# One program, two orders: VectorE's instructions in the step of an attention pass that has a ranking beside it

## The chip, the core and the metric

The kernel runs on one NeuronCore of one Trainium2 chip. The metric is the time of one execution on the device in microseconds. Five engines work side by side, each in the order of its own program: TensorE (PE; its weight loads are shown as PEld), VectorE (DVE), ScalarE (ACT), GpSimd (POOL) and SyncE (SP), which here only starts transfers. They wait for each other through semaphores: counters that an instruction raises when it ends, and that another waits on.

## The reference, cut to what matters

Four graph networks follow each other on 6250 nodes and 100000 edges, each with a residual and a layer norm. The first has two attention layers, of which the second (one head of 64 columns) is the stage that the change is in:

```
def _gat_layer(x, src, dst, W, a_src, a_dst, b, num_nodes):
    h = (x @ W).reshape(num_nodes, H, C)
    al_s, al_d = einsum(h, a_src), einsum(h, a_dst)
    logits = leaky_relu(al_s[src] + al_d[dst], 0.2)
    alpha = segment_softmax(logits, dst)        # exp(logits - max of the segment) / sum
    out = segment_sum(h[src] * alpha, dst)
...
x = layernorm(x + L0(x, edges))    # two layers like the above, edges grouped by dst
x = layernorm(x + L1(x, edges))    # two heads, edges grouped by src
x = layernorm(x + L2(x, edges))    # dot product attention, edges grouped by src
x = layernorm(x + L3(x, edges))    # two graph convolutions with batch norm
```

The kernel itself puts the edges in an order by windows of 128 nodes, once by dst and once by src, before it can sum over segments.

## The kernel before, in words

Nodes are held in 49 windows of 128. Edges are put into groups of 128, each belonging to one window; there are 832 groups, and eight of them make a batch, so an attention pass has 104 batches. For a batch, GpSimd gathers 8 x 128 table rows by indirect DMA, TensorE fetches each edge's node values by a matmul with a one-hot matrix (`of_node`), VectorE forms the logits (`meet`, `leak`), takes running maxima along and across the groups (`join`, `scan_forward`, `scan_back`, `row_scan_forward`, `row_scan_back`, `drop`, `widen`, `top`), with small transposes by TensorE between (`flat`, `ends`, `columns`, `back`), subtracts the maximum (`subtract`), ScalarE takes two exponentials (`weights`), VectorE multiplies the gathered rows by them (`weigh`, in four pairs), TensorE sums each group over the edges (`sums`), and VectorE adds each of the eight results to its window's accumulator (`add`, which waits for the add before it). The result of a group's add lies in a window whose number VectorE reads into registers once in four batches.

The order of all this is written out by hand, in one function per engine: `step` for TensorE, ScalarE and VectorE, `fetch` for SP. A step t handles pieces of four batches: the logits and maxima of batch t, the weighing and the first adds of batch t - 1, the last adds of t - 2, and the one-hot `turn` of t + 2.

In the second attention pass (stage `a2e`) another work runs beside it: the ranking of the edges by src, 98 batches of eight chunks of 128 edges (`SteppedRanking`, object `r`). Batch u of it runs in step t = u + 5 (LAG = 5). For it VectorE makes one-hot rows (`r.turn`, `r.mark_windows`), compares (`r.alike`), reads out what TensorE counted (`r.find_slot`, `r.find_column`, `r.find_row`) and then marks, for each of the eight chunks k, the column of every edge (`r.mark_column`, line L698: 128 x 832 elements, for TensorE's `put`, line L736). ScalarE compares (`r.compare`, L582) and makes the signs of the rows (`r.step_rows`, L706). TensorE does `r.starts` and `r.earlier` around `flat`, puts 0 and 1 of batch u - 1 behind `ends`, 2 and 3 behind `columns`, and 4 to 7 last in its step. VectorE's order in this stage is `step_beside`; the change touches nothing else.

SP's `fetch_both(t)` starts the place row of batch t, then waits until VectorE has done `top` of batch t - 2 (semaphore `s_peak`), and only then starts the flags, turns and the ranking's three transfers and goes on to the next step's place row. `turn(t + 2)` on VectorE waits for such a place row.

Lines on which the argument rests: L1639 `top` (writes `peak`), L1569 `sum_parts`, L1650 `subtract` (`argument`), L614 `r.alike`, L698 `r.mark_column`, L1544 `weigh`, L1556 `add`, L1575 and L1577 `meet`, L1583 `leak`, L1588 `join`, L1609 and L1614 the scans, L1533 `turn`, L1619 and L1624 the row scans, L680, L684, L690 and L691 the three `r.find`, L602 `r.turn`, L607 `r.mark_windows`, L1634 `widen`.

## Time and profile before

| what | value |
|---|---|
| median of 3 executions | 8981.2 us (8963.2 to 8990.8) |
| profiled execution: its time, its span | 8990.8 us, 8988.0 us |
| VectorE busy | 5885.6 us, 65% |
| TensorE busy | 5885.0 us, 65% |
| GpSimd busy | 5907.3 us, 66% |
| ScalarE busy | 4187.7 us, 47% |
| stage with the ranking beside it | about 2346 to 3581 us |

Busy shares over the whole span are averages over some twenty stages that have different limits, so none of them says what the stage of the change is bound by; this is read from the stage's own stretch. A row of the waits names the instruction that waited and what it waited for, as far as semaphore events show it; the time is idle time of the engine just before the instruction.

### The profile page before, as it was taken

The page shows a single profiled execution, that of the slowest core. Times are in us where ns is not written, and L with a number is a line of the kernel's source. Part 1 is how long each engine was busy: PE and PEld are TensorE (multiplying, and loading weights), DVE is VectorE, ACT ScalarE, POOL GpSimd, SP SyncE. Part 2 cuts the span into 40 slices and gives each one's busy share as a digit, 9 for nine tenths or more (in the row PEclk, how much of TensorE's full clock was granted, in tenths as well). Part 3 has the DMA queues.
Part 4 walks back from the last instruction along what each step waited for, and adds up shares of the span by engine and source line. Part 5 has one row for each costly group of instructions (what it writes and reads, how often), then busy time and mean ns, then how long its engine had stood idle before and what let it go on. Part 6 is the DMA issues. An engine that isn't in the chain of part 4 may idle for free. (4 is left out here: it accounts for less than half of the span.)

```text
span 8988.0 us, 137581 instructions
## 1 busy us (share of the span) xinstructions
PE 5885.0 (65%) x32642; PEld 4068.4 (45%) x32642; DVE 5885.6 (65%) x17613; ACT 4187.7 (47%) x12362; POOL 5907.3 (66%) x6034
## 2 busy tenths in 40 slices
PE   5776667777688787577776777777764444433336
PEld 3343344554555555344444445555453333333335
DVE  8998788888588887566666799899862222211113
ACT  6897533333477676333333344444433333333332
POOL 7897377775577665177774266666647777577773
PEclk9998867777578777777777899899985555555557
DMA  1333245553244443244443366566521222111111
GB/s 47 111 116 106 73 131 136 136 135 104 75 102 104 113 99 89 73 132 132 132 132 102 127 177 174 170 173 173 173 73 53 53 53 53 40 27 27 27 27 40
DMA packets 518706, 903.05 MB, mean 100 GB/s; under 512 B 149411, under 2 KB 258877, under 8 KB 517564
## 3 DMA queue, kind: packets, MB, share of 16 engines
q0 software_dynamic: 226304, 550.69, 23.5%
q1 hardware_dynamic: 291644, 343.69, 12.6%
q8 instruction: 301, 4.93, 0.2%
q14 instruction: 457, 3.74, 0.1%
HBM read 820.41 MB, written 73.07 MB: 99 GB/s over the span
## 5 line engine op out<-in xcount | busy, mean ns | idle before, releaser
L1292 POOL DMA_INDIRECT all_Y<-table,all_row x3328 | 3250.0, 977 | 1543.0 <-issue 956.0
L1835 POOL DMA_INDIRECT all_Y<-table,all_row x1664 | 1574.0, 946 | 547.5 <-issue 506.8
L1851 PE MATMUL g1e_ps_u<-all_Y,g1e_onehot 128*128 128x128 f32 x1664 | 428.8, 439 | 620.0 <-DMA all_Y<-table,all_row 452.8
L1851 PE MATMUL g2e_ps_u<-all_Y,g2e_onehot 128*128 128x64 f32 x1664 | 406.5, 426 | 641.2 <-DMA all_Y<-table,all_row 592.6
L1343 PE MATMUL be_ps_u<-all_Y,be_onehot 128*128 128x258 f32 x1664 | 655.7, 549 | 258.9 <-DVE all_acc L1556 252.4
L1879 DVE TENSOR_TENSOR all_acc<-all_acc,g1e_ps_u 128x128 f32 x832 | 238.8, 287 | 812.1 <-PE g1e_ps_u L1851 705.7
L1879 DVE TENSOR_TENSOR all_acc<-all_acc,g2e_ps_u 128x64 f32 x832 | 183.6, 221 | 866.3 <-PE g2e_ps_u L1851 759.7
L1343 PE MATMUL a1e_ps_u<-all_Y,a1e_onehot 128*128 128x264 f32 x1664 | 706.1, 554 | 5.1 <-DVE all_acc L1556 3.2
L1851 PEld LDWEIGHTS g1e_ps_u<-all_Y,g1e_onehot 128*128 128x128 f32 x1664 | 370.5, 328 | 678.2 <-issue 339.5
L1851 PEld LDWEIGHTS g2e_ps_u<-all_Y,g2e_onehot 128*128 128x128 f32 x1664 | 370.5, 328 | 677.3 <-issue 349.2
L1343 PEld LDWEIGHTS be_ps_u<-all_Y,be_onehot 128*128 128x128 f32 x1664 | 395.5, 266 | 483.6 <-issue 352.9
L1324 PE MATMUL te_ps_q<-all_X,te_turned 128*128 x1664 | 509.2, 435 | 154.4 <-DVE te_product L1594 131.6
L1343 PE MATMUL te_ps_u<-all_Y,te_onehot 128*128 128x264 f32 x1664 | 534.6, 437 | 74.3 <-DVE all_Y L1544 73.4
L638 POOL TENSOR_SCALAR all_acc<-all_Y,all_acc 128x128 f16<-128x128 f16 x392 | 489.4, 1259 | 45.1 <-DVE all_acc L625 35.1
L736 PE MATMUL a2e_rank_ps_p<-all_X 128*128 128x512 f16 (+1 forms) x1568 | 466.8, 449 | 0.2
L1324 PEld LDWEIGHTS te_ps_q<-all_X,te_turned 128*128 128x128 f32 x1664 | 330.5, 213 | 288.9 <-issue 244.0
L1343 PEld LDWEIGHTS a1e_ps_u<-all_Y,a1e_onehot 128*128 128x128 f32 x1664 | 383.4, 261 | 86.5 <-issue 14.1
L671 PE MATMUL rank_dst_ps_p<-all_acc 128*128 128x512 f16 (+1 forms) x1568 | 349.5, 344 | 106.8 <-POOL all_acc L638 106.5
L698 DVE TENSOR_SCALAR all_X<-all_Y,all_acc 128x832 f16<-128x832 f16 x784 | 385.6, 492 | 35.3 <-PE a2e_rank_ps_p L736 35.3
L1864 ACT ACTIVATE g1e_onehot<-g1e_distance 128x1024 f32<-128x1024 f16 x104 | 109.8, 1056 | 638.5 <-PE g1e_ps_u L1851 638.3
L1864 ACT ACTIVATE g2e_onehot<-g2e_distance 128x1024 f32<-128x1024 f16 x104 | 109.9, 1056 | 638.2 <-PE g2e_ps_u L1851 638.1
L1556 DVE TENSOR_TENSOR all_acc<-all_acc,te_ps_u 128x264 f32 x832 | 346.1, 416 | 82.5 <-issue 54.8
(555 smaller groups left out, 15616.4 us busy)
## 6 DMA issues: line engine op xcount, KB each, us to landing
all_Y<-table,all_row POOLq DMA_INDIRECT x4992
a1e_place_row<-places_dst SPq DMA_DIRECT2D x104, 256.0 KB
a2e_place_row<-places_dst SPq DMA_DIRECT2D x104, 256.0 KB
be_place_row<-places_src SPq DMA_DIRECT2D x104, 256.0 KB
te_place_row<-places_src SPq DMA_DIRECT2D x104, 256.0 KB
all_Y<-lows_dst SPq DMA_DIRECT2D x98, 256.0 KB
all_Y<-codes_dst SPq DMA_DIRECT2D x98, 256.0 KB
all_acc<-lows_src SPq DMA_DIRECT2D x98, 256.0 KB
```

Source lines behind the costliest of these rows:

```text
L638: pool.tensor_scalar(self.row1[b][:, k, :], self.kept.half16, self.row[b][:, k:k + 1], self.kept.other_t[:, t * 8 + k:t * 8 + k + 1], ALU. ...
L671: last = pe.matmul(ps[:, 0:a1 - a0], self.row1[b][:, k, :], self.column1[b][:, k, a0:a1], start=first, stop=final)
L698: dve.tensor_scalar(self.column1[b][:, k, :], self.kept.lane16, self.column[b][:, k:k + 1], self.kept.other_t[:, t * 8 + k:t * 8 + k + 1], ...
L736: last = pe.matmul(ps[:, 0:a1 - a0], self.row1[b][:, k, :], self.column1[b][:, k, a0:a1], start=first, stop=final)
L1292: pool.indirect_dma_start(out=rows[:, r, k, :], out_offset=None, in_=table, in_offset=bass.IndirectOffsetOnAxis(ap=order.row[:, t * 8 + k: ...
L1324: last = pe.matmul(ps_q[pair % 2][:, j * HC:(j + 1) * HC], turned[b][:, k * P:(k + 1) * P], queries[:, bass.ds(windows.at(windows_j, chunk ...
L1343: pe.matmul(ps_u[k % 4][:, 0:R], onehot[b][:, k, :], summand[:, b, k, :], start=True, stop=True).then_inc(s_summed, 1)
L1556: dve.tensor_tensor(mine, mine, ps_u[k % 4][:, 0:R], ALU.add).then_inc(s_added, 1)
L1835: pool.indirect_dma_start(out=rows[:, r, k, :], out_offset=None, in_=table, in_offset=bass.IndirectOffsetOnAxis(ap=order.row[:, t * 8 + k: ...
L1851: last = pe.matmul(ps_u[u][:, k * width:(k + 1) * width], onehot[b][:, k, :], rows[:, r, k, :], start=True, stop=True)
L1864: act.activation(onehot[t % MARKS][:, :, :], distance[:, :, :], ACT.Relu, scale=-1.0, bias=1.0).then_inc(s_onehot, 1)
L1879: dve.tensor_tensor(mine, mine, ps_u[(t - 1) % AHEAD][:, k * width:(k + 1) * width], ALU.add).then_inc(s_added, 1)
```

## The change

Only the order of VectorE's instructions in `step_beside` is changed. The marks of a ranking batch, which stood one by one between other instructions (0 and 1 at the end of a step, 2 to 7 spread over the first half of the next), now stand in pairs: 0 and 1 behind `widen`, 2 and 3 behind `top` of the same step, 4 and 5 in front of `scan_forward` of the next, 6 and 7 in front of its `row_scan_forward`. `weigh` of pair 0 becomes the first instruction of a step, the adds 4 to 7 stand between the short instructions of `meet`, `leak` and `join`, `turn(t + 2)` and `r.turn` move behind `r.find_row`, and `r.alike` in front of `subtract`.

```
                     if t == 0:
                         sum_parts(t, b)
-                    if late:
-                        r.mark_column(dve, u - 1, 2)
+                    weigh(t - 1, n, rp, 0)
                     add(t - 2, 4, -12, j)
-                    if late:
-                        r.mark_column(dve, u - 1, 3)
+                    meet(t, b, ring)
                     add(t - 2, 5, -11, j)
-                    weigh(t - 1, n, rp, 0)
-                    meet(t, b, ring)
+                    weigh(t - 1, n, rp, 1)
                     leak(t, b)
-                    if late:
-                        r.mark_column(dve, u - 1, 4)
-                    weigh(t - 1, n, rp, 1)
+                    add(t - 2, 6, -10, j)
                     join(t, b)
-                    add(t - 2, 6, -10, j)
-                    if late:
-                        r.mark_column(dve, u - 1, 5)
                     add(t - 2, 7, -9, j)
                     weigh(t - 1, n, rp, 2)
                     if late:
-                        r.mark_column(dve, u - 1, 6)
+                        r.mark_column(dve, u - 1, 4)
+                        r.mark_column(dve, u - 1, 5)
                     scan_forward(t, b)
                     fade_first(t - 1, n, -8, j)
-                    if late:
-                        r.mark_column(dve, u - 1, 7)
                     scan_back(t, b)
                     add(t - 1, 0, -8, j)
                     weigh(t - 1, n, rp, 3)
-                    turn(t + 2, b)
+                    if late:
+                        r.mark_column(dve, u - 1, 6)
+                        r.mark_column(dve, u - 1, 7)
                     row_scan_forward(t, b)
                     if now:
                         r.find_slot(dve, u)
                     add(t - 1, 1, -7, j)
                     row_scan_back(t, b)
-                    if then:
-                        r.turn(dve, u + 1)
                     if now:
                         r.find_column(dve, u)
                     add(t - 1, 2, -6, j)
                     drop(t, b)
                     if now:
                         r.find_row(dve, u)
+                    turn(t + 2, b)
                     add(t - 1, 3, -5, j)
                     if then:
+                        r.turn(dve, u + 1)
                         r.mark_windows(dve, u + 1)
                     widen(t, b)
                     if now:
                         r.mark_column(dve, u, 0)
+                        r.mark_column(dve, u, 1)
                     top(t, b)
+                    if now:
+                        r.mark_column(dve, u, 2)
+                        r.mark_column(dve, u, 3)
                     sum_parts(t + 1, n)
-                    if now:
-                        r.mark_column(dve, u, 1)
-                    subtract(t, b)
                     if then:
                         r.alike(dve, u + 1)
+                    subtract(t, b)
```

VectorE, from the writing of the peak over the end of one step into the next, before. In these rows "ISA" is an instruction on registers, which makes the address of the add behind it; the line numbers shown are the same in both programs.

```order
L1639 SCALAR_TENSOR_TENSOR a2e_peak<-a2e_flags,a2e_ps_r,a2e_widened 9x128
L1569 TENSOR_REDUCE a2e_spread<-a2e_ps_n 128x16
L698 TENSOR_SCALAR all_X<-all_Y,all_acc 128x832
L1650 TENSOR_TENSOR a2e_argument<-a2e_argument,a2e_ps_r 128x16
L614 TENSOR_TENSOR all_acc<-all_acc,all_Y 128x1024
L698 TENSOR_SCALAR all_X<-all_Y,all_acc 128x832
L1556 ISA
L1556 TENSOR_TENSOR all_acc<-all_acc,a2e_ps_u 128x66
L698 TENSOR_SCALAR all_X<-all_Y,all_acc 128x832
L1556 ISA
L1556 TENSOR_TENSOR all_acc<-all_acc,a2e_ps_u 128x66
L1544 TENSOR_TENSOR all_Y<-all_Y 128x2x64
```

The same place in the changed program:

```order
L1639 SCALAR_TENSOR_TENSOR a2e_peak<-a2e_flags,a2e_ps_r,a2e_widened 9x128
L698 TENSOR_SCALAR all_X<-all_Y,all_acc 128x832 x2
L1569 TENSOR_REDUCE a2e_spread<-a2e_ps_n 128x16
L614 TENSOR_TENSOR all_acc<-all_acc,all_Y 128x1024
L1650 TENSOR_TENSOR a2e_argument<-a2e_argument,a2e_ps_r 128x16
L1544 TENSOR_TENSOR all_Y<-all_Y 128x2x64
L1556 ISA
L1556 TENSOR_TENSOR all_acc<-all_acc,a2e_ps_u 128x66
L1575 TENSOR_TENSOR a2e_raw<-a2e_spread,all_Y 128x8
L1577 TENSOR_TENSOR a2e_argument<-a2e_spread,all_begins 128x8
L1556 ISA
L1556 TENSOR_TENSOR all_acc<-all_acc,a2e_ps_u 128x66
```

The first weighing (L1544) has moved up to directly behind the subtraction (L1650), and the two adds have short instructions between them and no mark.

VectorE, around the forward scan and the old place of `turn`, before:

```order
L1556 TENSOR_TENSOR all_acc<-all_acc,a2e_ps_u 128x66
L1544 TENSOR_TENSOR all_Y<-all_Y 128x2x64
L698 TENSOR_SCALAR all_X<-all_Y,all_acc 128x832
L1609 SCALAR_TENSOR_TENSOR a2e_forward<-a2e_flags,a2e_ps_l 9x128
L1564 ISA
L1564 TENSOR_TENSOR all_acc<-all_acc,a2e_fade 128x66
L698 TENSOR_SCALAR all_X<-all_Y,all_acc 128x832
L1614 SCALAR_TENSOR_TENSOR a2e_local<-a2e_flags,a2e_forward 9x128
L1556 TENSOR_TENSOR all_acc<-all_acc,a2e_ps_u 128x66
L1544 TENSOR_TENSOR all_Y<-all_Y 128x2x64
L1533 TENSOR_SCALAR a2e_turned<-a2e_place_row,all_lane_p 128x1024
L1619 SCALAR_TENSOR_TENSOR a2e_row_forward<-a2e_turns,a2e_ps_r 1x18
```

The same place in the changed program:

```order
L1556 TENSOR_TENSOR all_acc<-all_acc,a2e_ps_u 128x66
L1544 TENSOR_TENSOR all_Y<-all_Y 128x2x64
L698 TENSOR_SCALAR all_X<-all_Y,all_acc 128x832 x2
L1609 SCALAR_TENSOR_TENSOR a2e_forward<-a2e_flags,a2e_ps_l 9x128
L1564 ISA
L1564 TENSOR_TENSOR all_acc<-all_acc,a2e_fade 128x66
L1614 SCALAR_TENSOR_TENSOR a2e_local<-a2e_flags,a2e_forward 9x128
L1556 TENSOR_TENSOR all_acc<-all_acc,a2e_ps_u 128x66
L1544 TENSOR_TENSOR all_Y<-all_Y 128x2x64
L698 TENSOR_SCALAR all_X<-all_Y,all_acc 128x832 x2
L1619 SCALAR_TENSOR_TENSOR a2e_row_forward<-a2e_turns,a2e_ps_r 1x18
```

A mark no longer stands between the two scans, two stand where `turn` was. `turn` is now here, shortly before `widen`, in the changed program:

```order
L691 TENSOR_SCALAR all_acc<-all_acc 128x8
L1533 TENSOR_SCALAR a2e_turned<-a2e_place_row,all_lane_p 128x1024
L1556 ISA
L1556 TENSOR_TENSOR all_acc<-all_acc,a2e_ps_u 128x66
L602 TENSOR_SCALAR all_acc<-all_acc,all_lane_p 128x1024
L607 TENSOR_TENSOR all_acc<-all_Y 128x392
L1634 SCALAR_TENSOR_TENSOR a2e_widened<-a2e_flags,a2e_ps_r,a2e_local 9x128
L698 TENSOR_SCALAR all_X<-all_Y,all_acc 128x832 x2
L1639 SCALAR_TENSOR_TENSOR a2e_peak<-a2e_flags,a2e_ps_r,a2e_widened 9x128
```

Before, the same piece had neither L1533 nor L602 in it and one mark (L698) between L1634 and L1639 where there are two now.

## Rows read from the trace of the kernel before

**Rows 1.** Busy time by stretch (us; instructions), then clock, DMA share, GB/s.
```profile
core 0: us, PE busy (x) PEld busy (x) DVE busy (x) ACT busy (x) POOL busy (x), PEclk, DMA share, GB/s
2430.00:3560.00 1130.00, 934.27 (x8250) 627.26 (x8250) 979.91 (x4026) 822.60 (x2679) 801.90 (x769) 0.78 0.42 103
```

**Rows 2.** VectorE's waits from 2430 to 3560: total us, times, longest.
```profile
DVE a2e_turned L1533 <- DMA a2e_place_row<-places_dst: 47.9, 37, 15.3
DVE a2e_forward L1609 <- PE a2e_ps_l L1350: 40.4, 45, 1.6
DVE all_X L698 <- PE a2e_rank_ps_p L736: 35.3, 24, 1.8
DVE a2e_widened L1634 <- PE a2e_ps_l L1368: 14.4, 43, 0.7
DVE a2e_argument L1650 <- PE a2e_ps_r L1374: 6.5, 40, 0.2
```

**Rows 3.** TensorE's and ScalarE's waits in the same stretch.
```profile
ACT all_acc L582 <- DMA all_acc<-records: 178.8, 95, 3.7
...
PE a2e_ps_r L1358 <- DVE a2e_local L1614: 84.1, 93, 1.4
...
PE a2e_ps_r L1374 <- DVE a2e_peak L1639: 17.2, 44, 0.5
```

**Rows 4.** Timeline, VectorE, two steps: start us, duration us, instruction, [idle before].
```profile
2696.23 0.34 DVE L1639 SCALAR_TENSOR_TENSOR a2e_peak<-a2e_flags,a2e_ps_r,a2e_widened 9x128 f32<-9x128 bf16 x1
...
2701.32 0.40 DVE L1609 TENSOR_TENSOR_SCAN a2e_forward<-a2e_flags,a2e_ps_l 9x128 f32<-9x128 bf16 x1
...
2703.20 0.49 DVE L1533 TENSOR_SCALAR a2e_turned<-a2e_place_row,all_lane_p 128x1024 bf16<-128x1024 f16 x1 [0.31 <-DMA a2e_place_row<-places_dst]
...
2707.06 0.34 DVE L1639 SCALAR_TENSOR_TENSOR a2e_peak<-a2e_flags,a2e_ps_r,a2e_widened 9x128 f32<-9x128 bf16 x1
...
2713.69 0.41 DVE L1609 TENSOR_TENSOR_SCAN a2e_forward<-a2e_flags,a2e_ps_l 9x128 f32<-9x128 bf16 x1 [1.21 <-PE a2e_ps_l L1350]
...
2718.68 0.34 DVE L1639 SCALAR_TENSOR_TENSOR a2e_peak<-a2e_flags,a2e_ps_r,a2e_widened 9x128 f32<-9x128 bf16 x1
```

**Rows 5.** Timeline, TensorE, the same two steps.
```profile
2696.71 0.20 PE L1374 MATMUL a2e_ps_r<-all_ident,a2e_peak 9*128 9x9 f32 x1 [0.39 <-DVE a2e_peak L1639]
...
2700.39 0.27 PE L1350 MATMUL a2e_ps_l<-all_ident,a2e_joined 128*9 128x128 f32 x1 [0.36 <-DVE a2e_joined L1588]
...
2707.77 0.27 PE L1374 MATMUL a2e_ps_r<-all_ident,a2e_peak 9*128 9x9 f32 x1
...
2713.31 0.27 PE L1350 MATMUL a2e_ps_l<-all_ident,a2e_joined 128*9 128x128 f32 x1
```

**Rows 6.** Busy time by stretch, with the granted clock, in these steps.
```profile
2697.00:2702.00 5.00, 4.28 (x61) 3.32 (x61) 5.00 (x22) 3.92 (x13) 3.77 (x5) 1.00 0.68 174
2703.00:2706.00 3.00, 3.00 (x20) 1.83 (x17) 2.76 (x13) 2.50 (x9) 2.32 (x3) 0.50 0.16 26
2708.00:2713.00 5.00, 5.00 (x35) 3.27 (x34) 4.39 (x18) 3.70 (x11) 3.77 (x5) 0.50 0.67 156
```

**Rows 7.** Timeline, VectorE: alike, the register read's gap, a mark and an add.
```profile
2901.77 0.67 DVE L614 TENSOR_TENSOR all_acc<-all_acc,all_Y 128x1024 f16<-128x1024 f16 x1
2903.88 0.49 DVE L698 TENSOR_SCALAR all_X<-all_Y,all_acc 128x832 f16<-128x832 f16 x1 [1.44 <-PE a2e_rank_ps_p L736]
2904.29 0.22 DVE L1556 TENSOR_TENSOR all_acc<-all_acc,a2e_ps_u 128x66 f32 x1
```

**Rows 8.** Timeline, VectorE, the stage's early steps, without the ranking.
```profile
2371.71 0.17 DVE L1650 TENSOR_TENSOR a2e_argument<-a2e_argument,a2e_ps_r 128x16 f32<-128x16 f32 x1 [0.31 <-PE a2e_ps_r L1374]
2372.26 0.29 DVE L1544 TENSOR_TENSOR all_Y<-all_Y 128x128 f32<-128x128 f32 x1 [0.38 <-ACT all_Y L1468]
...
2379.30 0.23 DVE L1556 TENSOR_TENSOR all_acc<-all_acc,a2e_ps_u 128x66 f32 x1
2379.73 0.22 DVE L1556 TENSOR_TENSOR all_acc<-all_acc,a2e_ps_u 128x66 f32 x1 [0.21 <-PE a2e_ps_u L1343]
```

**Rows 9.** L1544 in the first attention pass, 1200 to 2200 us: idle before it, times.
```profile
PE a1e_ps_u L1343: 24.2, 12
issue: 24.1, 12
```

## The prediction

> **What bounds the kernel now.** I read the page's slices first (no engine is busy throughout, and different stages have different limits), then the table by stretches for the one stage that the change touches. It is the second attention pass with the ranking beside it, from about 2346 to 3581 us, 104 steps. The stretch from 2430 to 3560 us has both works in it and 96 steps, so a step takes 1130 / 96 = 11.77 us; VectorE is busy for 979.9 of the 1130 us, TensorE for 934.3, at a mean granted clock of 0.78 [rows 1]. VectorE and TensorE hand work back and forth in every step, so I then read whom VectorE waits for [rows 2], whom TensorE waits for [rows 3], and two whole steps in order of time [rows 4, 5].
>
> The reader is to see two segments. Segment A runs from the end of `peak` (L1639) to the start of the forward scan (L1609): TensorE transposes the peak back, does sums, four puts, and the next step's node and start matmuls, then the `flat` transpose (L1350) that the scan needs. Segment B runs from the forward scan to the end of the next `peak`; in it VectorE sets the pace and TensorE waits for it.
> - Segment A took 2701.32 - 2696.57 = 4.75 us where VectorE had no wait, and 2713.69 - 2707.40 = 6.29 us in the next step, with 1.21 us of waiting for `flat` [rows 4]. TensorE took 3.95 us from back to the end of `flat` in the first (0.36 of it a wait for `joined`) and 5.81 us in the second [rows 5]. The clock granted was 1.00 (2.4 GHz) there and 0.50 (1.2 GHz) here; it fell between the two, while TensorE waited for `local` [rows 6]. So A is VectorE's at the fast level and TensorE's at the slow one: VectorE waited there in 45 of 96 steps, 40.4 us in all [rows 2].
> - Segment B took 2719.02 - 2713.69 = 5.33 us without a wait [rows 4]. TensorE always arrives first in it: it waits for `local` in 93 of 96 steps, 84.1 us [rows 3].
>
> VectorE's own work is thus 4.75 + 5.33 = 10.08 us of the 11.77. The rest per step: 0.37 for the read of window numbers into registers (35.3 us, every fourth step; the view names TensorE's puts as releaser, but those are two steps old), 0.50 for the place row's DMA, 0.42 for `flat`, 0.15 for the fall's columns, 0.07 for the back transpose [rows 2], and 0.18 of slips under 0.15 us each. That makes B on average 5.33 + 0.50 + 0.15 + 0.09 = 6.07 and A the other 5.70.
>
> **The change part by part.** No instruction is added or removed; only VectorE's order changes. PE, ACT, POOL and SP keep theirs.
>
> 1. *Marks move from A to B.* A held marks 1 to 6, now it holds 2 to 5; B held 7 and 0, now 6, 7, 0, 1. A mark takes 0.41 us from its start to the next one's (2904.29 - 2903.88) [rows 7]. A's own work becomes 4.75 - 0.82 = 3.93, B's 5.33 + 0.82 = 6.15. (Two marks in a row might be up to 0.02 cheaper each; I count nothing.)
>
> 2. *The first weighing now stands right behind the subtraction.* It needs both exponentials of ScalarE, which need the subtraction's result. Before, alike, two marks and two adds lay between. The stage's early steps, which have no adds yet, show the naked price: argument starts at 2371.71, the weighing at 2372.26 with 0.38 us of idle time, where an instruction without a wait would have started some 0.08 before the end of the one ahead (2904.29 against 2903.88 + 0.49): 0.46 [rows 7, 8]. In 24 steps the register read stands there and covers it. Bounds: 0 (ScalarE's work hidden after all) to 0.46 in 72 steps; I take 0.46. Queued behind it are all of VectorE's adds, and `joined`, which TensorE's flat waits for.
>
> 3. *Register read behind a short instruction.* It now follows the subtraction (0.17 us), not alike (0.68). The gap was 1.44 behind alike [rows 7]; in the first attention pass, where it follows the subtraction, it is (24.2 + 24.1) / 24 = 2.01 [rows 9]. Bounds 1.44 and 2.01; I take 2.0, since that is the same order. The Trainium skill (DMA: Bandwidth & Descriptors, section "Latency and other measured facts") gives a load into registers a floor of about 0.6 us; by that figure alone the 24 gaps would be 1.4 us shorter each, some 33 us less, but both places in this trace are far above it, and the sum does not use it.
>
> 4. *Adds lose the mark that lay between them.* Each add waits for the add before it. Where two stand together the second starts 2379.73 - 2379.30 = 0.43 us after the first, with 0.21 of idle [rows 8]. In the new order the instructions between adds 4 and 5 fill about 0.29 us, between 6 and 7 about 0.23, between 1 and 2 about 0.31. That costs 0.14 + 0.20 in A and 0.12 in B. Bounds: nothing (if my count of filler is short) to these 0.46 a step; I take them.
>
> 5. *`turn(t + 2)` moves from behind the fourth weighing to behind find_row.* It waited for the place row's DMA in 37 steps, 47.9 us [rows 2]. SP issues that DMA only once it has seen the peak of the step before, so its arrival stands still against `peak`, while turn comes later: it started 2703.20 - 2701.32 - 0.31 = 1.57 us behind the scan [rows 4], and will start about 3.3 us behind it (two marks and eight short instructions more), 1.7 us later. One wait is 15.3 us long (two large loads stand in the queue ahead of that place row), the other 36 have a mean of (47.9 - 15.3) / 36 = 0.9. The long one keeps 13.6, of the others I keep 4 of 32.6 us: some 18 us stay, 30 go. Bounds: none goes, all 47.9 go.
>
> 6. *Waits for the fall's columns* (14.4 us in B) *and for back* (6.5 us, in A) [rows 2] go: between drop and widen there are now 0.8 us more work, and behind `peak` two marks and alike.
>
> New B: 6.15 + 0.12 + 18 / 96 = 6.46 against 6.07: +0.39 x 96 = **+37 us**. New A: where TensorE is late (45 steps) its time stands; where it was not, VectorE needs 3.93 + 0.46 + 0.34 = 4.73 instead of 4.75; in the 24 steps with a register read 3.93 + 2.0 + 0.34 = 6.27 instead of 4.75 + 1.44 = 6.19. There is one gain: TensorE waited for `peak` in only 44 steps [rows 3]; in the other 52 it came to the back transpose late, 0.37 instead of 0.14 us behind peak (2707.77 - 2707.40 against 2696.71 - 2696.57) [rows 4, 5]. With the longer B it is there in time: 0.23 x 52 = -12, +2 for the register steps (0.08 x 24), and -1 for the steps that were VectorE's: **-11 us**. Last, ScalarE: it waits for the record's DMA, 1.9 us in the mean and 3.7 at the longest [rows 3]; where that is latest its exponentials come later than the 0.46 above, now without cover. My estimate is eight steps by 0.4: **+3 us**. Together +37 - 11 + 3 = **+29 us**, in a profiled execution of 8990.8 us (span 8988.0): 9020. That execution is the slowest of the three; the median is 8981.2, so the forecast is **9010 us**, +0.3%.
>
> A difference under 0.3% (27 us) is about what a measurement of this kernel cannot tell from none, so this forecast stands on that border.
>
> **The rivals.**
> - *R1, the adds' spacing costs nothing, and the sum is near zero.* For it: my count of filler is rough, and VectorE may fetch ahead while an add waits. Against it: the 0.43 us stands in the trace with the same form of add. Then B is (6.34 - 6.07) x 96 = +26, A loses another 0.34 in the some 40 steps where VectorE sets it (-11 - 14 = -25), ScalarE +3: +4, so 8985 us.
> - *R2, the clock.* Segment B gets longer with the same matmuls in it, so TensorE is idler there; the trace has it at 0.50 right after such idle time [rows 6]. My new A is (5.70 x 96 - 11 - 24 x 6.27) / 72 = 5.36 us in a step without a register read. If each of these began at 1.2 GHz, it would be the second step's 6.29 less the late 0.23, 6.06: +0.70 x 72 = +50 on top of +29, so 9060 us. Against it: B's mean is 6.46 against 6.07, and most of the old B's waits were idle time as well. The Trainium skill (TensorE: Matmul & The Clock Gate, section "Why this matters for your kernels") says that idle gaps between bursts of matmuls bring the clock back to its lower level; by that rule the change leans this way.
> - *R3, faster: the place row was the real brake.* Were segment A to follow VectorE alone (TensorE at 2.4 GHz more often because the idle time before `local` shrinks by the mark that stood there, 0.41 of its 84.1 / 93 = 0.9 us), a step would be 4.73 + 6.27 and the register steps 1.54 more: 72 x 11.0 + 24 x 12.54 + 18 = 1111 us, against 1130: -19, so 8962 us; with the adds' 0.46 free as well -63, 8918 us. It decides once A, in the steps without a register read, falls below (1130 - 96 x 6.46 - 24 x 6.27) / 72 = 4.99 us, from the 5.36 above. Against it: TensorE's own matmuls in A are the same, 3.6 us at 2.4 GHz but 5.8 at 1.2 [rows 5].
> - *R4, the order does nothing because TensorE's chain absorbs it.* It would need B to be TensorE's; it waits there in 93 of 96 steps, so I give it little and count it under "same".
>
> **How the numbers follow.** Forecast case, +29 with +-15: 0.42. R1 0.22. R2 0.18. R3 0.12. R4 0.06. The forecast case lies half above the 0.3% bound; with all of R2 and a share of R1 that gives slower 0.46. Same: a bit under half of the forecast case, most of R1 and R4, part of R3: 0.38. Faster: 0.16. The likeliest case's own range is 8995 to 9025; the range for 8 in 10 reaches down into R3 and up into R2: 8952 to 9068.
>
> **What would show it.** In the profile after: the first weighing waits for ACT L1468 in about 70 steps, 0.3 to 0.4 us each; the idle time by the register read goes from 1.44 to 2.0; the wait for the place row falls to 15 to 20 us, those for the columns and for back to nearly nothing; the wait for `flat` grows from 40 to about 60 us or more, since VectorE comes to the scan sooner; TensorE's wait for `peak` appears in nearly all steps; steps of about 12.05 us. I am wrong if the stretch of both works is shorter than before, if the weighing does not wait, or if the clock in it leaves 0.75 to 0.80.

## The result, and the profile after

The kernel after takes 9038.8 us in the median of four runs (9013.1 to 9043.2), the kernel before 8984.0 on the same chip (8963.2 to 8990.8): a ratio of 1.0064 with a 95% interval of 1.0049 to 1.0080, so some 57 us slower. The forecast was 9010 us, +29 us, with a range of 8952 to 9068; the direction held, and half of the size is missing in it. The profiled execution of after took 9060.3 us (span 9058.5).

The stretch with both works in it, now 1206 us long for the same 769 gathers [rows 1 have 1130 for them]:

```profile
core 0: us, PE busy (x) PEld busy (x) DVE busy (x) ACT busy (x) POOL busy (x), PEclk, DMA share, GB/s
2430.00:3636.00 1206.00, 973.21 (x8257) 661.26 (x8256) 988.14 (x4029) 824.04 (x2680) 971.97 (x769) 0.74 0.39 96
```

VectorE has 8 us more to do and ScalarE 1; it is GpSimd whose busy time went from 801.9 to 972.0 us, with as many instructions. VectorE's waits there (total us, times, longest), against [rows 2]:

```profile
DVE a2e_forward L1609 <- PE a2e_ps_l L1350: 67.2, 70, 1.7
DVE a2e_raw L1575 <- DMA all_Y<-table,all_row: 59.0, 19, 4.5
DVE all_Y L1544 <- ACT all_Y L1468: 52.3, 96, 1.1
DVE a2e_turned L1533 <- DMA a2e_place_row<-places_dst: 14.3, 1, 14.3
DVE a2e_widened L1634 <- PE a2e_ps_l L1368: 0.7, 1, 0.7
```

and TensorE's, against [rows 3]:

```profile
PE a2e_ps_r L1374 <- DVE a2e_peak L1639: 129.1, 91, 16.0
PE a2e_ps_r L1358 <- DVE a2e_local L1614: 19.5, 64, 0.9
```

Four of these lines are what the prediction asked for: the wait for `flat` grew from 40 to 67 us, the place row's shrank to its one long piece, the one for the columns is gone, and TensorE is in time for `peak` in 91 of 96 steps instead of 44. The weighing (L1544) does wait for ScalarE, in 96 steps where some 70 were expected. The second line, `meet` (L1575) waiting for the gathered rows up to 4.5 us at a time, was in no part of the prediction. So I read GpSimd, which has only gathers to issue in this stage: before, then after, 2430 to 3540 us, with count, busy time, mean ns of one, and idle time ahead of them.

```profile
L1292 POOL DMA_INDIRECT all_Y<-table,all_row x767 | 799.8, 1043 | 310.2 <-issue 205.7 <-DVE all_Y L1544 104.5
```
```profile
L1292 POOL DMA_INDIRECT all_Y<-table,all_row x707 | 896.1, 1268 | 215.4 <-issue 196.8 <-DVE all_Y L1544 18.6
```

One gather instruction takes 1.27 us in the mean instead of 1.04, and 0.30 us passes between two. Eight a step need 8 x (1.043 + 0.30) = 10.7 us before, of a step of 11.77, and 8 x (1.268 + 0.30) = 12.54 after, where the step, from the sixth forward scan of the stage to the last, is (3642.62 - 2410.92) / 98 = 12.57. GpSimd used to wait for VectorE (104.5 us) and hardly does any longer (18.6 us): it is what bounds the stage. One of its long instructions and its neighbours (start, us):

```profile
2552.67 1.19 POOL L1292 DMA_INDIRECT all_Y<-table,all_row  x1 [0.30 <-issue]
2554.16 3.57 POOL L1292 DMA_INDIRECT all_Y<-table,all_row  x1 [0.30 <-issue]
2558.04 0.94 POOL L1292 DMA_INDIRECT all_Y<-table,all_row  x1 [0.30 <-issue]
```

VectorE at the same time:

```profile
2554.23 0.88 DVE L698 TENSOR_SCALAR all_X<-all_Y,all_acc 128x832 f16<-128x832 f16 x2
2555.05 0.34 DVE L1639 SCALAR_TENSOR_TENSOR a2e_peak<-a2e_flags,a2e_ps_r,a2e_widened 9x128 f32<-9x128 bf16 x1
2555.31 0.89 DVE L698 TENSOR_SCALAR all_X<-all_Y,all_acc 128x832 f16<-128x832 f16 x2
2556.12 0.19 DVE L1569 TENSOR_REDUCE a2e_spread<-a2e_ps_n 128x16 f32<-128x48 f32 x1
2556.24 0.67 DVE L614 TENSOR_TENSOR all_acc<-all_acc,all_Y 128x1024 f16<-128x1024 f16 x1
2556.84 0.15 DVE L1650 TENSOR_TENSOR a2e_argument<-a2e_argument,a2e_ps_r 128x16 f32<-128x16 f32 x1
...
2557.58 0.21 DVE L1556 TENSOR_TENSOR all_acc<-all_acc,a2e_ps_u 128x66 f32 x1
2560.72 0.17 DVE L1575 TENSOR_TENSOR a2e_raw<-a2e_spread,all_Y 128x8 f32<-128x8 f32 x1 [2.92 <-DMA all_Y<-table,all_row]
```

The gather that began at 2554.16 ended at 2557.73, 0.89 us behind 2556.84, the start of the first instruction behind the row mark 0, mark 1, `top`, mark 2, mark 3, sum, alike. An undisturbed one takes 0.94 in all, so this one seems to have done its work when the row was over. All 39 gathers over 3 us in the stretch end 0.88 to 0.91 us behind the start of that instruction. VectorE then waits 2.92 us for the late rows of the table.

### The profile page after: what moved, and what is told of

Its sections match the earlier page's. It is cut to its first block and busy times, and to the rows that moved or that the text cites. A ratio compares the mean times of both kernels' runs of the same rounds, so it can differ in the third digit from the quotient of the medians.

```text
span 9058.5 us, 137581 instructions
## 1 busy us (share of the span) xinstructions
PE 5911.9 (65%) x32642; PEld 4085.2 (45%) x32642; DVE 5896.6 (65%) x17613; ACT 4188.0 (46%) x12362; POOL 6066.1 (67%) x6034
## 5 line engine op out<-in xcount | busy, mean ns | idle before, releaser
L1292 POOL DMA_INDIRECT all_Y<-table,all_row x3328 | 3413.4, 1026 | 1469.4 <-issue 966.4
L1830 POOL DMA_INDIRECT all_Y<-table,all_row x1664 | 1570.1, 944 | 548.8 <-issue 506.5
L1544 DVE TENSOR_TENSOR all_Y<-all_Y 128x128 f32<-128x128 f32 (+1 forms) x728 | 377.7, 519 | 74.3 <-ACT all_Y L1468 54.6
L671 PE MATMUL rank_dst_ps_p<-all_acc 128*128 128x512 f16 (+1 forms) x1568 | 352.1, 347 | 104.5 <-POOL all_acc L638 104.1
L1343 PE MATMUL a2e_ps_u<-all_Y,a2e_onehot 128*128 128x66 f32 x1664 | 350.7, 348 | 90.8 <-DVE all_acc L1556 90.6
```

The source lines that it names most:

```text
L671: last = pe.matmul(ps[:, 0:a1 - a0], self.row1[b][:, k, :], self.column1[b][:, k, a0:a1], start=first, stop=final)
L1292: pool.indirect_dma_start(out=rows[:, r, k, :], out_offset=None, in_=table, in_offset=bass.IndirectOffsetOnAxis(ap=order.row[:, t * 8 + k: ...
L1343: pe.matmul(ps_u[k % 4][:, 0:R], onehot[b][:, k, :], summand[:, b, k, :], start=True, stop=True).then_inc(s_summed, 1)
L1544: dve.tensor_tensor(out[:, :, :, 0:C], rows[:, r, ks, value_c0:value_c0 + HC].rearrange("p k (h n) -> p k h n", h=H), bc(by, [P, 2, H, C]) ...
L1830: pool.indirect_dma_start(out=rows[:, r, k, :], out_offset=None, in_=table, in_offset=bass.IndirectOffsetOnAxis(ap=order.row[:, t * 8 + k: ...
```

## The experiments

Two readings were set against each other. V: the loss is VectorE's own order, as predicted. P: VectorE's rows of marks, that is several of them one directly behind the other, slow GpSimd's gathers. From f2 on P has a sharper form, R: any unbroken row of marks and of operations with two inputs in SBUF (the core's working memory) holds a gather until the row is over. Each run below stands beside its own measurement of the kernel before, which lay between 8962 and 8977 us and not at 8984; so where an expectation names a time, compare its distance from before. The table holds all twelve runs; "step" is from the sixth forward scan to the last by 98, "need" is what GpSimd's gathers take of a step by their mean length and 0.30 us, "L1575" the waits for late rows over the whole stage, its beginning included.

| kernel | ratio to before (95%) | step | need | gather mean | L1575: us, times |
|---|---|---|---|---|---|
| before | 1 | 11.77 | 10.74 | 1.043 | 12.2, 3 |
| after | 1.0064 (1.0049, 1.0080) | 12.57 | 12.54 | 1.268 | 72.6, 23 |
| e1_marks_back | 1.0017 (1.0007, 1.0026) | 11.85 | 11.83 | 1.179 | 46.1, 16 |
| e2_marks_alone | 1.0103 (1.0088, 1.0119) | 12.60 | 12.56 | 1.270 | 49.3, 14 |
| e3_no_pairs | 1.0024 (1.0014, 1.0035) | 11.87 | 11.16 | 1.095 | 13.4, 3 |
| e4_weigh_later | 1.0092 (1.0077, 1.0107) | 12.49 | 12.49 | 1.261 | 87.8, 25 |
| f1_one_gather_off | 1.0029 (1.0020, 1.0038) | 11.95 | 10.68 (seven) | 1.226 | 5.7, 1 |
| f2_alike_behind | 1.0109 (1.0093, 1.0124) | 12.62 | 12.60 | 1.275 | 95.9, 28 |
| f3_turn_late | 0.9958 (0.9944, 0.9971) | 11.28 | 10.96 | 1.070 | 14.9, 5 |
| f4_marks_behind_top | 0.9967 (0.9955, 0.9979) | 11.33 | 10.89 | 1.061 | 13.2, 5 |
| g1_weigh_first | 0.9953 (0.9940, 0.9967) | 11.28 | 10.98 | 1.073 | 13.2, 3 |
| g2_alike_ahead | 0.9961 (0.9948, 0.9975) | 11.44 | 11.36 | 1.120 | 25.2, 10 |
| g3_slot_ahead | 0.9930 (0.9917, 0.9944) | 11.06 | 10.66 | 1.032 | 12.7, 4 |
| g4_both | 0.9955 (0.9942, 0.9969) | 11.37 | 11.09 | 1.086 | 12.4, 3 |

**e1_marks_back**, after with the marks alone put back:

```
 weigh 0
+mark 2
 add 4
+mark 3
 meet, add 5, weigh 1, leak
+mark 4
 add 6, join
+mark 5
 add 7, weigh 2
-mark 4, mark 5
+mark 6
 scan_forward, fade_first
+mark 7
 scan_back, add 0, weigh 3
-mark 6, mark 7
...
-mark 0, mark 1
+mark 0
 top
-mark 2, mark 3
 sum_parts
+mark 1
 alike, subtract
```

> Kernel after, with the eight marks alone put back to where the kernel before has them relative to the scans and products (each by itself, marks 2 and 3 in the next step, behind the weighing); the weighing first, the adds spread, the late turn and alike ahead of subtract stay. Theory P (pairs): in the trace of after GpSimd's gather instructions take 1.6 to 2.0 us where they lie beside two marks in a row and 3.4 to 3.6 us beside four, and in 23 steps the logit addition (L1575) then waits 2.4 to 4.5 us for the gather; with the marks apart these go, so 8980 to 9005 us, GpSimd's mean gather back at 1.05 us, and the wait at L1575 under 15 us. Theory V (VectorE's own order, as predicted: ScalarE's weights waited for, register read, adds bound to each other): all of these stay, so 9020 to 9045 us.

8977.9 us beside 8962.2, +16 us: three quarters of the loss go with the marks' place, as P has it, and V's range is missed. But the mean gather is 1.179, not 1.05, and 16 late ones stay: pairs are not the whole of it, and step and need still agree (11.85, 11.83).

**e2_marks_alone**, before with the marks where after has them:

```
-mark 2
 add 4
-mark 3
 add 5, weigh 0, meet, leak
-mark 4
...
+mark 4, mark 5
 scan_forward
...
 weigh 3
+mark 6, mark 7
...
+mark 1
 top
+mark 2, mark 3
 sum_parts
-mark 1
 subtract, alike
```

> Kernel before, with the marks alone put where the kernel after has them (4 and 5 ahead of the forward scan, 6 and 7 behind the fourth weighing, 0 and 1 ahead of top, 2 and 3 behind it); nothing else moved. Theory P: the pairs alone do it, so 9025 to 9060 us, gather instructions of up to 3.6 us, and waits of over 2 us at L1575 in some 20 steps. Theory V: the weighing still stands behind two adds and waits little, the two marks moved give the stretch ahead of the scan what they take from the one behind it, so 8965 to 9000 us.

9053.2 beside 8962.2, +91 us. P's time holds as it was stated; by its distance from before it is more than P expected, and more than the whole change costs. The long gathers are there (up to 3.73 us), the waits over 2 us fewer than the some 20 expected (12). V's range is missed.

**e3_no_pairs**, after's stretches, but one short instruction between any two marks:

```
-mark 4, mark 5, scan_forward, fade_first, scan_back, add 0, weigh 3, mark 6, mark 7
+mark 4, add 7, weigh 2, mark 5, scan_forward, fade_first, mark 6, scan_back, add 0, mark 7, weigh 3
...
-widen, mark 0, mark 1, top, mark 2, mark 3, sum_parts, alike
+mark 0, widen, mark 1, top, mark 2, sum_parts, mark 3, alike
```

> Kernel after, with the marks in the same stretches of the step (four around widen and top, four around the forward scan) but never two in a row: one short instruction between any two (0 widen 1 top 2 sum 3 alike, and 4 seventh-eighth add 5 forward scan and fade 6 backward scan and add 7). Theory P: GpSimd gets in between two marks, the gathers of 3.4 us and the 23 late ones go, so 8990 to 9015 us. Theory V: VectorE does the same work in the same two stretches, one mark more is even put between forward scan and its successors, so 9030 to 9060 us.

8985.2 beside 8962.2, +23 us: by this distance P's range, not V's. GpSimd needs only 11.16 of the 11.87 us here, so what is left of the loss, 23 us, is VectorE's.

**e4_weigh_later**, after without the wait for ScalarE:

```
-weigh 0, add 4, meet, add 5, weigh 1
+add 4, meet, add 5, weigh 0, weigh 1
```

> Kernel after, with the first weighing alone moved behind add 4, meet and add 5, so that it no longer waits for ScalarE's weights (54.6 us over the 102 steps of the last stage in the profiled run). Theory P: VectorE is not what binds; the 0.4 us a step are waited elsewhere (for the flat scan input or the gather), so 9025 to 9045 us, within 15 us of after. Theory V: the wait is on the path in some 80 steps, so 35 us less than after: 8995 to 9010 us.

The wait for ScalarE went from 54.6 us (102 times) to 0.2, and the kernel is no faster: 9042.9 beside 8962.2, +81 us where after has +57, so more than the 15 us apart that P allowed. The step is about as long (12.49 against 12.57 us). More is waited for the gather instead (87.8 us against 72.6). Taking away the weighing's wait, one of the prediction's largest terms, buys nothing while GpSimd bounds the stage.

**f1_one_gather_off**, after with GpSimd relieved of an eighth of its work:

```
 for k in range(8):            # GpSimd
+    if beside is not None and k == 7:
+        continue
...
+apart(sp, s_summand, (t - RING) * BY_DVE + 4, s_passed_sp)      # SyncE
+sp.dma_start(rows[:, j % RING, 7, :], table[0:P, :]).then_inc(s_eighth[j % RING], 16)
```

> Kernel after with VectorE's order untouched; in the last stage GpSimd issues seven of a batch's eight gathers, and the eighth tile is filled by a plain transfer of the table's first 128 rows, issued by SyncE. It leaves out the gather of the eighth chunk (its rows are not the ones the reference wants). Theory P (GpSimd, slowed by rows of marks, has become the bound): the gather instructions still reach 3.5 us, but seven a step by about 1.6 us each make 11 us, under the step of 12, so the late gathers at L1575 go (under 15 us in all) and the time is at most 25 us over before. Theory V (VectorE's own order): nothing on VectorE has changed, so 45 to 65 us over before, as after.

8991.6 beside 8966.3: +25 us, ratio 1.0029, at the edge of P's range and far from V's. VectorE's order is after's to the letter, gathers of 3.58 us are still there, and no step with both works in it has a late one. VectorE's waits over the stage (all line numbers are 8 higher than in after, L1583 is `meet`; the one late gather lies ahead of the ranking):

```profile
DVE a2e_forward L1617 <- PE a2e_ps_l L1358: 74.8, 83, 1.7
DVE all_Y L1552 <- ACT all_Y L1476: 54.4, 102, 1.1
...
DVE a2e_raw L1583 <- DMA all_Y<-table,all_row: 5.7, 1, 5.7
```

**f2_alike_behind**, after with `alike` behind `subtract`:

```
-sum_parts, alike, subtract
+sum_parts, subtract, alike
```

> Kernel after with alike (L614, the product of two f16 tiles, 0.67 us) alone put back behind subtract. In the trace of after a gather that starts inside marks 0, 1, top, marks 2, 3, sum, alike ends about 0.9 us behind the start of the instruction that follows alike, as if it did all its work then. Theory R (an unbroken row of marks and of operations with two inputs in SBUF holds the gather until the row is over): without alike in the row the longest gathers fall from 3.5 to about 2.9 us, and the time is 20 to 45 us over before, less than after. Theory M (only the marks and turns hold it): the longest stay at 3.4 us or fall to the length of the marks alone, 1.9 + 0.9 = 2.8, while a row ending in alike leaves no trace in after; the time stays within 10 us of after's 57 over before.

9062.8 beside 8966.3, +97 us: both expectations missed, the one in time as well as in length (the longest gather is 3.86 us). The trace fits R's rule all the same: `alike` now runs straight into the weighing, which no longer waits, so the row is longer, not shorter.

```profile
2502.30 0.89 DVE L698 TENSOR_SCALAR all_X<-all_Y,all_acc 128x832 f16<-128x832 f16 x2
2503.12 0.34 DVE L1639 SCALAR_TENSOR_TENSOR a2e_peak<-a2e_flags,a2e_ps_r,a2e_widened 9x128 f32<-9x128 bf16 x1
2503.38 0.89 DVE L698 TENSOR_SCALAR all_X<-all_Y,all_acc 128x832 f16<-128x832 f16 x2
2504.20 0.19 DVE L1569 TENSOR_REDUCE a2e_spread<-a2e_ps_n 128x16 f32<-128x48 f32 x1
2504.31 0.15 DVE L1650 TENSOR_TENSOR a2e_argument<-a2e_argument,a2e_ps_r 128x16 f32<-128x16 f32 x1
2504.39 0.67 DVE L614 TENSOR_TENSOR all_acc<-all_acc,all_Y 128x1024 f16<-128x1024 f16 x1
2504.99 0.28 DVE L1544 TENSOR_TENSOR all_Y<-all_Y 128x128 f32<-128x128 f32 x1
2505.20 0.20 DVE L1556 TENSOR_TENSOR all_acc<-all_acc,a2e_ps_u 128x66 f32 x1
```

GpSimd's gather beside it:

```profile
2502.31 3.78 POOL L1292 DMA_INDIRECT all_Y<-table,all_row  x1 [0.30 <-issue]
```

It ends at 2506.09, again 0.89 us behind the start of the instruction that follows the row (2505.20), and the weighing is now part of the row. So it is in 12 of the 19 gathers over 3 us; in the other 7 the read of window numbers parts `alike` from the weighing by 1.1 us, and the gather ends 0.83 us behind the end of `alike`. The two instructions within the row that read PSUM, where TensorE's results lie (L1569, L1650, 0.1 us each from start to start), let nothing in here.

**f3_turn_late**, before with one move of the change:

```
-weigh 3, turn(t + 2), row_scan_forward
+weigh 3, row_scan_forward
...
-find_row, add 3
+find_row, turn(t + 2), add 3
```

> Kernel before with one edit of the change alone: turn(t+2) moved from behind the fourth weighing to behind find_row. Its wait for the place row (50.4 us, 39 times, in the last stage of before) shrinks to about 20 us. All theories: gain if the wait was on the path; 15 to 35 us less than before. Theory P adds that the turn then stands closer to marks 0 and 1 and may lengthen a gather; the mean gather stays under 1.1 us, so it costs nothing.

8927.4 beside 8966.3, -39 us: a bit more than the range. Its waits:

```profile
DVE all_X L698 <- PE a2e_rank_ps_p L736: 35.6, 24, 1.8
DVE a2e_row_forward L1619 <- PE a2e_ps_r L1359: 32.6, 104, 0.7
...
DVE a2e_forward L1609 <- PE a2e_ps_l L1350: 22.3, 39, 1.4
DVE a2e_turned L1533 <- DMA a2e_place_row<-places_dst: 18.6, 3, 15.1
```

**f4_marks_behind_top**, f3 with each of marks 0 to 3 one place later:

```
-mark 2, add 4, mark 3, add 5, weigh 0
+add 4, mark 2, add 5, mark 3, weigh 0
...
-widen, mark 0, top, sum_parts, mark 1, subtract, alike
+widen, top, sum_parts, mark 0, subtract, mark 1, alike
```

> Kernel of the late turn (before with turn behind find_row), and marks 0, 1, 2 and 3 each moved one place later: 0 behind top and sum, 1 behind subtract, 2 behind add 4, 3 behind add 5, so each still stands by itself but mark 0 no longer lies between the forward scan and top (0.41 us off that stretch, 0.41 us more ahead of the next scan, where VectorE waits for TensorE in some 47 of 104 steps). Theory V: 10 to 20 us less than the late turn alone. Theory P: the same, if the mean gather stays under 1.1 us; mark 1 next to alike may cost some of it.

8929.8 beside 8966.3, the same as f3: missed. The segment from scan to peak is shorter (5.43 us in the mean instead of 5.77), but the other took it all (5.90 instead of 5.50).

**g1_weigh_first, g2_alike_ahead, g4_both** put the rest of the change on f3:

```
-mark 2, add 4, mark 3, add 5, weigh 0, meet, leak, mark 4, weigh 1, join, add 6, mark 5     (g1, g4)
+weigh 0, mark 2, add 4, mark 3, meet, add 5, weigh 1, leak, mark 4, add 6, join, mark 5
...
-mark 1, subtract, alike     (g2, g4)
+mark 1, alike, subtract
```

> Kernel of the late turn (38 us under before) with a second edit of the change: the first weighing at the head of the step and the adds spread as in after; marks by themselves, alike behind subtract as in before. Theory V, as the prediction had its largest term: the weighing waits 0.46 us for ScalarE in most steps, so 30 us more than the late turn (about 8 under before). Theory R (rows): alike (0.6 us) now stands between subtract and the weighing and covers ScalarE's work, so no wait; but mark 1, subtract, alike, weighing and mark 2 follow each other, a gather that begins in this row is held until its end, and GpSimd, whose eight gathers need 8 x (1.07 + 0.30) = 11.0 us of a step of 11.2 in the late turn's trace, becomes late: mean gather at least 1.12 us, some waits of over 2 us at L1575, 10 to 40 us more than the late turn.

> Kernel of the late turn with alike ahead of subtract instead, nothing else. Theory V: subtract is 0.6 us later, but two marks and two adds still lie between it and the weighing, so no wait for ScalarE: within 8 us of the late turn (38 under before). Theory R: mark 0, top, sum, mark 1, alike stand in a row of 1.9 us; gathers of 2.6 to 2.8 us appear, the mean gather is at least 1.12 us, some gathers are late at L1575: 15 to 40 us more than the late turn.

> Kernel of the late turn with both edits that alone cost at most 3 us: the weighing at the head of the step and alike ahead of subtract; it differs from the kernel with the marks put back (16 us over before) only in that the ranking's turn (L602) stays behind row_scan_back instead of standing between add 3 and mark_windows. Theory V, the prediction's largest term: nothing lies between subtract and the weighing any more, so the weighing waits about 0.4 us for ScalarE in 70 steps or more; 25 to 35 us more than the late turn (5 to 15 under before). Theory R: the ranking's turn is part of the row turn, add, turn, windows, widen, mark 0, top; with it away the mean gather falls from 1.18 to 1.12 us or less and the late gathers at L1575 from 15 to 9 or fewer, so the kernel is 15 to 35 us under the one with the marks put back. Neither excludes the other: if both hold, 5 to 15 us under before; if only V holds, 10 to 20 over before; if only R, 25 to 38 under.

All three cost nothing that can be told from f3: 8927.1 beside 8973.6, 8932.5 beside 8973.6, 8938.0 beside 8976.7. For g1 both theories expected a loss in some form and neither came. For g2 V was right and R was not: the mean gather did rise to 1.120, with ten waits for late rows, but the time hardly moved. In g4 R's numbers held (mean gather 1.086, three late waits), and V's 25 to 35 us did not come. The weighing's wait is there,

```profile
DVE all_Y L1544 <- ACT all_Y L1468: 31.4, 78, 1.0
...
DVE a2e_forward L1609 <- PE a2e_ps_l L1350: 13.8, 23, 1.1
```

but less is then waited for `flat` (13.8 against 22.3 us), and the kernel ends 39 us under before. g4 and e1 differ only in the ranking's turn (L602): behind row_scan_back in g4, between add 3 and mark_windows in e1, where turn, add 3, the ranking's turn, windows, widen, mark 0 and top follow each other. That move alone is 0.9955 against 1.0017, some 55 us, more than the 15 to 35 that R gave it.

**g3_slot_ahead**, f3 with find_slot in the wait of row_scan_forward:

```
-weigh 3, row_scan_forward, find_slot
+weigh 3, find_slot, row_scan_forward
```

> Kernel of the late turn with find_slot (L680, 0.53 us) moved ahead of row_scan_forward, which in the late turn's trace waits 0.3 us for TensorE's ends in each of 103 steps. Theory V: the wait is filled, 0.3 us a step, 20 to 30 us less than the late turn (60 to 70 under before). Theory R: GpSimd needs 11.0 us of the 11.2 of a step, so at most 0.2 us a step is to be had: 5 to 20 us less than the late turn, and waits for the gather at L1575 appear or grow.

8908.4 beside 8973.6, ratio 0.9930 (0.9917 to 0.9944): it beats both kernels, by V's number. R's cap did not bind, since the mean gather fell as well (1.032), which neither had expected.

## Why the prediction came out as it did

A path of single edits leads from before to after, and its ratios place the time: before 1, the late turn 0.9958 (-38 us), weighing first, adds spread and alike ahead 0.9955 (nothing), the ranking's turn behind add 3 1.0017 (+55), the marks in pairs and moved 1.0064 (+42). Each link is uncertain by some 15 us, and the chips of the runs differ.

- *"PE, ACT, POOL and SP keep theirs."* This sentence ahead of the six steps is what failed. Their orders do stay, but I took GpSimd's durations for fixed and never asked what the new rows on VectorE do to it. [Rows 1] had it busy for 801.9 us in 96 steps; with the 0.30 us between gathers that is 10.7 of 11.77 us, 9% from being the bound. The missing term is 769 x (1.268 - 1.043) = 173 us of GpSimd's work, of which some 100 fitted into its slack. It came out in segment A, from `peak` to the next forward scan: forecast 11 us shorter in all, it grew from 5.69 to 6.27 us in the mean of 98 steps, 57 us.
- *The sum for VectorE's order*, +29, is close to what f1 measured with that order and GpSimd relieved: +25 us, a step of 11.95 (e3, another order in the same segments: +23, 11.87). So about 25 of the 57 us are the mechanism of the prediction and about 30 GpSimd's. That split is an inference: f1 also changes who fetches the eighth tile. That the sum came so near is in part luck, since its parts did not all hold:
- *Step 1, marks from A to B*, held. A step of after without a late gather:

```profile
2513.39 0.41 DVE L1609 TENSOR_TENSOR_SCAN a2e_forward<-a2e_flags,a2e_ps_l 9x128 f32<-9x128 bf16 x1 [1.72 <-PE a2e_ps_l L1350]
...
2519.17 0.34 DVE L1639 SCALAR_TENSOR_TENSOR a2e_peak<-a2e_flags,a2e_ps_r,a2e_widened 9x128 f32<-9x128 bf16 x1
...
2520.97 0.15 DVE L1650 TENSOR_TENSOR a2e_argument<-a2e_argument,a2e_ps_r 128x16 f32<-128x16 f32 x1
2521.50 0.29 DVE L1544 TENSOR_TENSOR all_Y<-all_Y 128x128 f32<-128x128 f32 x1 [0.38 <-ACT all_Y L1468]
```

  B is 2519.51 - 2513.39 = 6.12 us, which is also the median; the forecast was 6.15, and 6.27 with the adds' term. With the place row's wait the mean is 6.28 where 6.46 was forecast.
- *Step 2, the weighing's wait*: the size held (0.38 us idle at 2521.50), the price did not. I charged 0.46 us in each of 72 steps, 33 us; e4 and g4 put it at nothing, once because GpSimd was the bound and once because `flat` was waited for less.
- *Step 3, the register read*: the idle time there was expected at 2.0 us; it is 1.00 to 1.05, under my lower bound of 1.44. The same read costs 39.1 us in 25 steps, 1.6 each, in g1, with alike ahead of it again, and 1.40 to 1.73 us for nearly all reads of g4, where it follows the subtraction as in after. What sets it stays open; a gap taken from another stage was a poor guide.
- *Step 4, dependent adds*: nothing of it is visible in B. Where I did put two adds side by side (e2), the second waited 0.22 us in the mean (45.0 us, 207 times); the filler in after was enough. My count of it was short, as R1 said.
- *Step 5, the place row's wait*, held: 14.3 us left against 18 forecast, and f3 shows it worth 39 us by itself against the 30 in the sum.
- *Step 6* held: 0.7 us are left of the wait for the columns, and the wait for back is gone from the stretch.
- *A*, and the time it was to give back, did not hold. The forecast was 5.59 us in the mean against 5.69 measured in before. In after 19 of 98 steps have a wait of 2.4 to 4.5 us for late rows in it, and there A takes 8.22 us; in the other 79 it still takes 5.80. With GpSimd relieved (f1) it is 5.65, a gain of 4 us in all where 11 were forecast.
- *R2, the clock*: it did fall, from 0.78 to 0.74, out of the 0.75 to 0.80 that I had named as a sign of being wrong. But with after's order and GpSimd relieved it is above before's:

```profile
2430.00:3540.00 1110.00, 872.33 (x7978) 594.35 (x7979) 952.89 (x3891) 795.34 (x2595) 809.07 (x660) 0.81 0.40 102
```

  So the longer B does not lower the clock. Over the same stretch it is 0.74 to 0.76 in the four kernels with a step of about 12.5 us or more (after, e2, e4, f2) and 0.78 to 0.81 in all others. What lowers it there stays open: in after it is 0.75 in the steps with a late gather and 0.74 in the others.
- *R3* had the place row as the real brake, and f3 shows for that edit alone that its wait was on the path (-39 us), though A fell only from 5.48 to 5.22 us in the steps without a register read, not below the 4.99 that R3 asked for. In after the wait is gone as well; that its gain is still there, under the two losses, is an inference.

The steps came to 12.57 us, not 12.05, and the clock left its bounds: by the prediction's own criteria the mechanism was incomplete. The total, 9038.8 us, lies outside the likeliest case's 8995 to 9025. It lies inside 8952 to 9068 by luck: that range reached so far up for R2, a clock lowered by the longer B, and what filled the room was GpSimd, for which the sum had nothing.

## What to carry to other kernels

When an edit moves only one engine's instructions, ask of every other engine not just whether its order changes but whether its durations can: here an engine that nobody waited for was 9% from being the bound. Compare the work that each engine needs per step (mean length plus the gap behind it, by the count) with the step itself; where they agree to 0.1 us, as in after, suspect that engine as the bound, and test it by giving it less to do before removing another engine's wait. Where GpSimd issues gathers and is near that point, try first to keep VectorE's large f16 instructions from SBUF to SBUF out of rows.

## What the runs showed of the hardware

- *In after, a gather instruction on GpSimd that begins inside the row of marks around `top` ends as if it did its work behind the row.* Alone it takes 0.94 us; in after 39 took 3.4 to 3.6 us, each ending 0.88 to 0.91 us behind the start of the instruction that follows the row, and f2's example the same. The Trainium skill (SBUF — State Buffer, section "SBUF: two separate sides") says that a VectorE instruction in a mode that uses both port pairs locks GpSimd out while it writes descriptors; the holds beside the marks, which are f16 to f16 in SBUF with per-partition scalars, agree with that, though the profile does not show an instruction's mode. Its section "Who interferes with whom" infers that an operation on two SBUF tensors does not disturb the writing of descriptors. Here such operations prolong the hold: the row went on through `alike` and, in f2, through the weighing. The gather also reads its row numbers from SBUF, which by the same section would contend; which of the two it is, no run here separates.
- *An operation with two inputs in SBUF holds a gather by itself.* In before 42 gathers begin while `alike` runs, with only the subtraction, which reads PSUM, ahead of it. They take 1.06 to 1.36 us, and each ends 0.82 us behind the end of `alike`, wherever in it they began. One of them, and VectorE beside it:

```profile
2477.95 1.32 POOL L1292 DMA_INDIRECT all_Y<-table,all_row  x1 [0.31 <-issue]
```
```profile
2477.76 0.68 DVE L614 TENSOR_TENSOR all_acc<-all_acc,all_Y 128x1024 f16<-128x1024 f16 x1
2478.36 0.49 DVE L698 TENSOR_SCALAR all_X<-all_Y,all_acc 128x832 f16<-128x832 f16 x1
```

- *What makes a row one hold stays open.* In 31 of these 42 a mark runs directly behind `alike`, as at 2478.36, and does not prolong the hold. And in before the subtraction between mark 1 and `alike` did let gathers in: 26 that began in mark 1, with the subtraction directly behind it, end 0.82 us behind the mark's end. So R's rule describes the long holds of after and f2, and not every neighbourhood.
- *Short breaks need not help.* In f2 `sum` and `subtract`, which read PSUM, did not let the waiting gather in. With the one-instruction spacing of e3 74 gathers between 2430 and 3540 us are over 1.5 us long, against 8 in before and 164 in after.
- *The cost is not in proportion to the time of what is moved.* Moving a single 0.47 us instruction (L602) in among windows, `widen`, mark 0 and `top` cost some 55 us over the kernel (e1 against g4), with the mean gather at 1.179 instead of 1.086 us.
